# A four-layer stack of attention, feed forward and state space: products with a zero state left out, one output product moved, loads and splits moved

## The chip, the core and the metric

One core of one Trainium2 chip runs the whole program in one launch. Its engines are TensorE (PE; its weight loads are PEld), VectorE (DVE), ScalarE (ACT), GpSimd (POOL) and SyncE (SP), which issues most DMAs. The metric is device time in microseconds (us), the median of several runs; lower is better.

## The reference

Two rows (b = 0, 1) of 1024 tokens by 512 features, float32, go through four layers, each `x = x + layernorm(f(layernorm(x)))`:

```python
att  = softmax(causal(q @ k.T / 4)); out = att @ v @ Wo.T + bo       # 32 heads of 16
ffn0 = lin(silu(lin(x, gate)) * lin(x, up), down)   # lin: w * (su @ sv), rank 4, 1792 wide
# state space: 8 groups of 8 heads of 64, state 128
xBC = silu(conv4(x @ Wx)); dt = softplus(x @ Wdt + dt_bias)
state = state * exp(dt * A) + dt * x * B            # state starts at zero
y = state @ C + x * D
out = (rmsnorm_by_group(y) * norm_weight * silu(x @ Wgate)) @ Wout
ffn1 = (silu(x @ Wg) * (x @ Wu)) @ Wd               # 1376 wide, padded to 11 tiles of 128
```

## The kernel before

**Products.** Most float32 products are three matmuls each: both operands are split into a rounded part ("hi") and a rest ("lo"), and hi·hi, lo·hi and hi·lo are summed in a PSUM bank. Weights come by DMA into a raw tile, ACT or POOL makes the hi part and POOL the lo part.

**Phases.** A loop runs over the two rows. In each, the engines pass the phases ATT, PROJ, FFN0, STEPS_DT, MAMBA and FFN1. An engine that is done with a phase drains and calls `leave`; an engine that calls `enter` waits until all five have left the phase before. Phases reuse SBUF, and that is what `enter` protects. Within a phase, each engine runs its own list of instructions in order, and semaphores connect them; nothing is reordered at run time.

**Attention.** Eight quads of four heads (t = 0 to 7). `attention_order` writes out one list, `ORDER`, that all engines follow. Its first part makes queries and keys ("proj", f = 0 to 3, four 512-token halves each) and values; among them stand "pieces", products of queries and keys for the row maxima of quad 0, which DVE reduces. A projection for f waits for the split of its weights (`wqk_ready`), which waits for their load (`load_qk(f)` in SP's list). Each quad's operands are then copied by 24 DMAs into `stack_q` and `stack_k` (`copy_part`): SP does this for quads 0, 1 and 2 (`stack`), ACT's queue for quad 3 (the "copies" entries). SP's list is: load f=0, 1; stack 0; load f=2; stack 1; wait for the values; ones; stack 2; load f=3; `put_maxima(0)`, two DMAs that bring the turned maxima into `stack_q`. The first score product waits for the latter, and the first exponential on ACT for all of stacks 2 and 3, because they are copied from the `probs` tiles that it writes.

**State space.** STEPS_DT makes the time steps: `steps_in(s)` is the product with Wdt for one half of the tokens, `steps_copy` brings it to SBUF, `steps_turn` turns it, and `decay_sums` forms the running sums. The phase also makes the first conv projections (`project`, `first_conv`, `first_silu`) and the second half of the layer norm (`normed_y`, `add_y`, `moments_x`, `root`, `normed_x`, `norm_turn`, `norm_lo`, in that order of need). SP loads Wdt and the small parameters after `enter(STEPS_DT)`, then `cpar` and the first weight tiles.

MAMBA runs eight groups (g), the middle six in a hardware loop, each in eight chunks of 128 tokens (c). `m_group` in each engine's part has the chunk's list. On PE: the decays, the B and C products into bank 3 (L998, L999), one or two conv projections for the next half or group (two at c = 0 and 2 of each half), into banks 0 and 1 in turn; the product of C with the state ("inter", L1020); the gate product, with the eight head products of the chunk between its matmuls (L959); the out projection of the chunk before (`project_out`, weights `wy`, with four transposes between); and the state's update product (L1046). The two banks of projections and gate are shared: a use waits until the use two before it has been read, a projection by DVE's `convolve`, so the gate of chunk 0 waits for the conv of the first projection. `turned_hi` (ACT, L1257) and `turned_lo` (DVE, L1711) copy the chunk before's normalised result, turned by PE (L940), out of bank 2; `project_out` waits for them. DVE sums y (L1764, L1767), gates it (L1769), adds the out projection to Y (`gather`, L1719) and updates the state (L1788); POOL decays the state (L2078). At the start of a group DVE sets the state to zero (L1739), and chunk 0 goes through the same operations with it as the others.

**Second feed forward.** SP loads its first two tiles after `enter(FFN1)`, POOL splits them, and PE starts with `gate(0, 0, 0)`. The second half of the norm runs beside it: after `moments_x` a `root` on POOL, then `normed_x` on ACT, and PE's `norm_turn` for tokens 4 to 7 stands behind its third product.

## Time and profile before

| | |
|---|---|
| median of 3 runs | 4067.1 us (4065.34 to 4072.07) |
| the profiled execution | 4082.54 us |
| its span | 4080.8 us |
| PE busy, matmuls | 3809.3 us (93%), 18088 |
| DVE busy | 2732.6 us (67%) |
| ACT busy | 1686.5 us (41%) |
| POOL busy | 1805.8 us (44%) |
| mean granted clock | 0.925 of 2.4 GHz |

A span is from the first to the last instruction of one profiled execution. Busy shares are means over phases with different limits. A matmul's end is modelled, so rows overlap a little: the time of a run of matmuls is the distance between two starts. SPq and ACTq are the issue times of DMAs in SP's and ACT's queue.

### The profile page before, as it was taken

How to read it: one execution, taken by the hardware profiler on the slowest of the kernel's cores; microseconds unless marked ns; L12 is line 12 of the kernel's file. 1: busy time of each engine (PE TensorE's matmuls, PEld its weight loads, DVE VectorE, ACT ScalarE, POOL GpSimd, SP SyncE). 2: the span in 40 equal slices, each digit the busy share in tenths (PEclk: the TensorE clock that was granted, in tenths of full speed). 3: DMA queues.
4: the chain of work that ended last, by engine and by line, in shares of the span. 5: the costliest groups of instructions: out<-in, count | busy, mean ns of one | idle time of the engine just before them, and what ended most of it. 6: DMA issues, size and time to landing. Idle time of an engine off the chain costs nothing.

```text
span 4080.8 us, 61636 instructions
## 1 busy us (share of the span) xinstructions
PE 3809.3 (93%) x18088; PEld 2768.1 (68%) x18088; DVE 2732.6 (67%) x5102; ACT 1686.5 (41%) x3555; POOL 1805.8 (44%) x1993
## 2 busy tenths in 40 slices
PE   7899899799999999979979998996999999999797
PEld 5444588577777777767754446874777777777586
DVE  4576455678777787764546754556778777787545
ACT  1344411355555555541214443114555555555412
POOL 2111444266555665643221124433666655665432
PEclk9767799899999999989987768998999999999899
DMA  4120111011010111001051301101111100110111
GB/s 104 31 49 27 34 48 40 24 37 35 29 27 25 31 36 28 23 26 57 24 116 27 61 15 33 48 32 34 27 37 31 31 21 25 36 34 18 52 39 36
DMA packets 84630, 151.95 MB, mean 37 GB/s; under 512 B 16488, under 2 KB 18616, under 8 KB 84432
## 3 DMA queue, kind: packets, MB, share of 16 engines
q1 hardware_dynamic: 80784, 142.23, 13.1%
q10 hardware_dynamic: 3648, 7.34, 0.7%
q8 instruction: 92, 1.51, 0.1%
q14 instruction: 106, 0.87, 0.1%
HBM read 119.37 MB, written 4.19 MB: 30 GB/s over the span
## 4 chain that ended last, share of the span: by engine, by line
PE 81%; issue 7%; DVE 4%; POOL 2%; DVEq 2%; ACT 1%; POOLq 1%; DMA 1%; SPq 1%; ACTq 0%; PEldq 0%; PEld 0%
PE banks L928 30%; PE banks L595 8%; PE banks L596 7%; PE banks L597 7%; PE banks L845 5%; PE banks L959 4%; PE banks L826 4%; PE banks L803 3%; PE banks L1020 2%; PE banks L1046 2%; PE banks L976 1%; PE banks L977 1%; PE banks L949 1%; PE banks L940 1%; DVEq L1690 1%
## 5 line engine op out<-in xcount | busy, mean ns | idle before, releaser
L1687 DVE SCALAR_TENSOR_TENSOR conv<-banks,cpar,conv 128x509 f32<-128x509 f32 (+2 forms) x576 | 428.1, 743 | 123.0 <-ACT conv L1247 106.0
L959 PEld LDWEIGHTS banks<-xdt,decay 128*128 128x128 f32 x2048 | 393.9, 193 | 65.8 <-DVE decay L1706 11.2
L1213 ACT ACTIVATE probs<-banks 128x1024 f32<-128x1024 f32 (+3 forms) x384 | 296.7, 809 | 328.9 <-PE banks L826 328.3
L1474 DVE TENSOR_TENSOR Y<-banks,Y 128x512 f32<-128x512 f32 x368 | 253.1, 691 | 164.3 <-PE banks L597 163.0
L595 PE MATMUL banks<-xhi,f_hi 128*128 128x512 f32 x800 | 325.8, 407 | 30.9 <-POOL f_lo L1891 16.6
L959 PE MATMUL banks<-xdt,decay 128*128 128x64 f32 x2048 | 342.0, 249 | 12.7 <-DVE decay L1706 9.3
L2012 POOL TENSOR_SCALAR_AFFINE_SELECT probs<-probs 128x256 f32<-128x256 f32 x256 | 103.8, 406 | 536.6 <-ACT probs L1213 536.2
L803 PE MATMUL banks<-stack_k,stack_q 48*128 48x512 f32 (+3 forms) x768 | 320.5, 500 | 13.8 <-DVE mx L1607 6.8
L1602 DVE CUSTOM_DVE_ANT_0 banks<-banks,mask_qk 128x128 f32<-128x128 f32 (+3 forms) x512 | 249.3, 500 | 117.7 <-PE banks L803 113.2
L596 PE MATMUL banks<-xhi,f_lo 128*128 128x512 f32 x800 | 320.8, 401 | 0.0
L597 PE MATMUL banks<-xlo,f_hi 128*128 128x512 f32 x800 | 320.6, 401 | 0.0
L928 PE MATMUL banks<-xhi,wx_hi 128*128 128x512 f32 x720 | 310.4, 431 | 0.0
L826 PE MATMUL banks<-stack_q,stack_k 50*128 50x512 f32 (+3 forms) x768 | 292.0, 487 | 5.7 <-DVE mx L1602 3.0
L928 PE MATMUL banks<-xhi,wx_lo 128*128 128x512 f32 x720 | 295.9, 411 | 0.0
L928 PE MATMUL banks<-xlo,wx_hi 128*128 128x512 f32 x720 | 295.5, 410 | 0.0
L826 PEld LDWEIGHTS banks<-stack_q,stack_k 50*128 50x128 f32 x768 | 169.0, 249 | 168.3 <-issue 125.8
L928 PE MATMUL banks<-wg_hi,xhi 128*128 128x512 f32 x512 | 262.0, 512 | 21.8 <-DVE conv L1687 21.8
L2090 POOL TENSOR_SCALAR rg<-ss 128x1 f32<-128x1 f32 x128 | 25.1, 196 | 541.3 <-ACT banks L1321 541.3
L1889 POOL TENSOR_SCALAR f_hi<-f_raw 128x512 fp32r<-128x512 f32 x150 | 96.5, 643 | 324.2 <-PE banks L597 301.9
L928 PE MATMUL banks<-wg_lo,xhi 128*128 128x512 f32 x512 | 238.3, 465 | 0.0
L1132 ACT CAST h_hi<-hf 128x512 fp32r<-128x512 f32 x100 | 62.2, 622 | 408.2 <-DVE hf L1459 408.2
L928 PE MATMUL banks<-wy_hi,yt_hi 128*128 128x512 f32 x512 | 229.4, 448 | 0.7 <-POOL wy_lo L2038 0.7
(229 smaller groups left out, 10402.1 us busy)
## 6 DMA issues: line engine op xcount, KB each, us to landing
m_raw<-in_w_mamba SPq DMA_DIRECT2D x224, 256.0 KB, 2.6
f_raw<-in_w_ffn SPq DMA_DIRECT2D x50, 768.0 KB, 4.6
x_next<-in_x SPq DMA_DIRECT2D x6, 1024.0 KB, 8.8
wqk_raw<-in_w_attn SPq DMA_DIRECT2D x8, 512.0 KB, 3.7
stack_q<-part_hi SPq DMA_DIRECT2D x64, 64.0 KB, 2.4
stack_k<-part_hi SPq DMA_DIRECT2D x64, 64.0 KB, 2.5
X<-in_x SPq DMA_DIRECT2D x4, 1024.0 KB, 6.5
out_y<-X ACTq DMA_DIRECT2D x4, 1024.0 KB, 5.1
```

The source lines that it names most:

```text
L595: pe.matmul(dst, a_hi(kt), w_hi(kt), start=first, stop=False)
L596: pe.matmul(dst, a_lo(kt), w_hi(kt), start=False, stop=False)
L597: return pe.matmul(dst, a_hi(kt), w_lo(kt), start=False, stop=last)
L803: pe.matmul(bank[RING_BANK[use]][:, 0:cols], stack_q[buf][base:base + ROWS, h, i * P:(i + 1) * P], stack_k[buf][base:base + ROWS, h, s * H ...
L826: r = pe.matmul(bank[h][:, at:at + w], stack_k[buf][base:base + ROWS + 2, h, j * P:(j + 1) * P], stack_q[buf][base:base + ROWS + 2, h, s * ...
L845: r = pe.matmul(bank[6][32 * h:32 * h + VW, lo:HALF], V[:, j, QUAD * t + h, :], probs[n % 2][:, h, at:at + w], start=j == 0, stop=j == CPH ...
L928: r = pe.matmul(dst, a(kt), w(kt), start=n == 0, stop=n == 3 * KT - 1)
L959: r = pe.matmul(bank[7][:, h * MP:(h + 1) * MP], decay[:, h, :], xdt[:, h * MP:(h + 1) * MP], start=True, stop=True, skip_group_check=True)
L1213: act.activation(probs[n % 2][:, 2 * p:2 * p + 2, 0:w], banks[:, 2 * p:2 * p + 2, 0:w], ACT.Exp, scale=1.0 / HD ** 0.5).then_inc(exp_done[ ...
L1474: dve.tensor_tensor(Y[:, i, :], bank[6 + i % 2], Y[:, i, :], ALU.add).then_inc(f["dn_used"], 1)
L1602: dve.tensor_tensor_reduce(out=src, in0=src, in1=mask_qk[:, HALF - cols:HALF], scale=1.0, scalar=NEG, op0=ALU.add, op1=ALU.max, accum_out= ...
L1687: r = dve.scalar_tensor_tensor(out=rest, in0=src[:, 0:HALF - lag], scalar=cpar[:, o:o + 1], in1=rest, op0=ALU.mult, op1=ALU.add)
```

## The change

The state space's chunk 0 of each group leaves out the product of C with the zero state, the eight scalings of it on ACT, one of DVE's two sums, the memset and POOL's decay of the state; the state after chunk 0 is a copy of the update product. In chunk 0 of each group but the first, the out projection of the chunk before stands ahead of the gate product, and `turned_hi` and `turned_lo` stand ahead of the first conv. The second feed forward's first two tiles are loaded as soon as the last group's projections are done, and POOL splits the first of them (three matrices) before it leaves MAMBA; tile buffers of the second feed forward lie elsewhere in SBUF for that. Wdt, the small parameters, `cpar` and the first two state space weight tiles are loaded before SP leaves FFN0, and Wdt is split at the end of POOL's FFN0 list. In STEPS_DT some steps change places. In attention, SP's list now has load f=3 right after stack 1 and copies quad 3 too, between stack 2 and `put_maxima(0)`; ACT copies nothing. The weights of queries and keys are split in one piece per f, after the last projection of f-1. The pieces stand four to a block, and a step with the maxima and six pieces stands between projections f=2 and f=3. The core of the diff:

```diff
-    blocks_left = [("values", 3), (1, 0), ("values", 4), (1, 1), ("values", 5), ("values", 6), (1, 2), ("values", 7),
-                   (1, 3), (2, 0), (2, 1), (2, 2), (2, 3), (3, 0), (3, 1), (3, 2), (3, 3)]
-    for at, (first, second) in enumerate(blocks_left):
+    blocks_left = [("values", 3), (1, 0), ("values", 4), (1, 1), ("values", 5), (1, 2), ("values", 6), (1, 3),
+                   ("values", 7), (2, 0), (2, 1), (2, 2), (2, 3), None, (3, 0), (3, 1), (3, 2), (3, 3)]
+    for block_ in blocks_left:
+        if block_ is None:
+            yield "maxima", 0
+            yield from some(2)
+            yield "maxima_out", 0
+            yield from some(AHEAD - 2)
+            continue
+        first, second = block_
...
+        count = min(PER_BLOCK, len(pieces) - (NQ - 1) * NP) if len(pieces) > (NQ - 1) * NP else 0
+        yield from some(min(count, 2))
         yield ("values_out", second) if values else ("proj_lo", first, second)
-        yield from some(count - 2 if count > 2 else 0)
+        yield from some(count - min(count, 2))
...
@@ SyncE, attention @@
         stack(0)
         load_qk(2)
         stack(1)
+        load_qk(3)
         held(sp, v_used, b + 1)
         ones_in(1)
         stack(2)
-        load_qk(3)
+        stack(3)
         put_maxima(0)
         for t in range(1, NQ):
...
@@ SyncE, ffn_loads @@
             load(0, 0, True)
             load(0, 1, True)
             if i == 1:
+                leave(sp, b, MAMBA)
+                enter(sp, b, FFN1)
...
@@ SyncE, end of FFN0 @@
         ffn_loads(0, w_ffn0, NF0, True)
-        leave(sp, b, FFN0)
-        enter(sp, b, STEPS_DT)
-
+        enter(sp, b, FFN0)
         for dst, src in ((wdt_raw[:], w_dt), (dtb[:], dt_bias), (alog[:], a_log), (dsk[:], d_skip)):
             sp.dma_start(dst, src).then_inc(dt_w_in, 16)
-        leave(sp, b, STEPS_DT)
-
+        sp.dma_start(cpar[:], conv_par[0]).then_inc(cpar_in, 16)
...
-        sp.dma_start(cpar[:], conv_par[0]).then_inc(cpar_in, 16)
-        for n in range(CT):
-            m_load(0, n, n, n < 2)
+        for n in range(2):
+            m_load(0, n, n, True)
+        leave(sp, b, FFN0)
+        enter(sp, b, STEPS_DT)
+        for n in range(2, CT):
+            m_load(0, n, n)
+        leave(sp, b, STEPS_DT)
...
         m_group(MG - 1, True)
-        leave(sp, b, MAMBA)
-        enter(sp, b, FFN1)
+        held(sp, proj_done, (b + 1) * PROJ_PER_B)
         ffn_loads(1, w_ffn1, NF1, False)
...
@@ TensorE, attention @@
-                if use_f % 2 == 0 and part == 0:
-                    pe.wait_ge(wqk_ready, b * 8 + 2 * f + which + 1)
+                if use_f == 0 and part == 0:
+                    pe.wait_ge(wqk_ready, b * 8 + 2 * f + 2)
...
@@ TensorE, m_group @@
-                pe.wait_ge(state_ready, it + 1)
-                if c == 0:
-                    pe.wait_ge(inter_used, START + it)
-                pe.matmul(bank[6][:], xbc[s][:, XT + 1, ck], state[:], start=True, stop=True
-                          ).then_inc(inter_done, 1)
+                if c:
+                    pe.wait_ge(state_ready, sm + c)
+                    pe.matmul(bank[6][:], xbc[s][:, XT + 1, ck], state[:], start=True, stop=True
+                              ).then_inc(inter_done, 1)
+
+                def out_ahead():
+                    if c == 1:
+                        pe.wait_ge(m_split, b * (MG * W_PER_G) + g * W_PER_G + W_PER_G)
+                    pe.wait_ge(bc_ready, START + it + 1)
+                    ahead = (c + 1) % CPH != 0
+                    project_out(it - 1, {2 + 2 * k: lambda k=k: turn_x(it + 1, c + 1, k) for k in range(XT)}
+                                if ahead else {})
+
+                if c == 0 and not start:
+                    out_ahead()
...
+                if c:
+                    out_ahead()
 
                 if c < TT - 1:
-                    pe.wait_ge(inter_used, START + it + 1)
+                    pe.wait_ge(inter_used, START + sm + c)
...
@@ TensorE, STEPS_DT @@
-            if ft == 2:
+            if ft == 1:
                 norm_turn(b * 4 + 2, 2, half(1))
                 normed(b * 4 + 2, 1)
                 steps_in(1)
-            if ft == 3:
+            if ft == 2:
                 steps_turn(1)
...
@@ ScalarE, attention, copies @@
-                first, last = arg
-                if first == 0:
-                    held(act, v_used, b + 1)
-                    held(act, part_lo_ready, b * 16 + 8)
-                    act.drain()
-                for n in range(first, last):
-                    copy_part(act, 3, n)
...
@@ ScalarE, m_group @@
+                if c == 0 and not start:
+                    turned_hi(it - 1)
...
                     if not turned_yet:
-                        turned_hi(it - 1)
+                        if c:
+                            turned_hi(it - 1)
...
+                if c:
+                    act.wait_ge(inter_done, START + (b * MG + g) * (TT - 1) + c)
+                    act.wait_ge(gt_ready, (b * MG + g) * 2 + c // CPH + 1)
+                    for h in range(HPG):
+                        own = slice(h * MP, (h + 1) * MP)
+                        r = act.activation(yv[:, own], bank[6][:, own], ACT.Identity, scale=gt[:, EC, c, h:h + 1])
+                    r.then_inc(inter_used, 1)
...
@@ ScalarE, STEPS_DT @@
+        act.wait_ge(dt_w_in, (b + 1) * 64)
+        act.activation(neg_a[:], alog[:], ACT.Exp)
         held(act, cpar_in, (b * MG + 1) * 16)
         for n in range(2):
             split_hi(wx_hi[:, n, :], n, 0)
-        act.wait_ge(dt_w_in, (b + 1) * 64)
-        act.activation(neg_a[:], alog[:], ACT.Exp)
         normed_y(b * 4 + 1, half(1))
         for n in range(2, 4):
             split_hi(wx_hi[:, n, :], n, 0)
         first_conv(0)
+        normed_x(b * 4 + 2, 2, half(1))
         first_conv(1)
         first_tanh(0)
-        normed_x(b * 4 + 2, 2, half(1))
...
@@ VectorE, m_group @@
-            held(dve, inter_done, START + (b * MG + g) * TT)
-            dve.memset(state[:], 0.0).then_inc(state_ready, 1)
...
+                if c == 0 and not start:
+                    turned_lo(it - 1)
+                    turned = True
...
+                if c == 0:
+                    dve.wait_ge(intra_done, START + it + 1)
+                    dve.wait_ge(pool_x, START + it + 1)
+                    dve.tensor_tensor(yv[:], xd[:], bank[7], ALU.add).then_inc(y_ready, 1)
...
+                if c == 0:
+                    dve.wait_ge(st_mm, START + sm + 1)
+                    dve.tensor_copy(state[:], bank[6]).then_inc(state_ready, 1)
...
@@ VectorE, STEPS_DT @@
+        steps_copy(0)
         add_y(b * 4 + 1, half(1))
         moments_x(b * 4 + 1, 1)
-        steps_copy(0)
         first_conv(0)
+        norm_lo(b * 4 + 2, half(1))
         first_conv(1)
         first_silu(0)
-        norm_lo(b * 4 + 2, half(1))
...
@@ GpSimd, ffn @@
-        split_one(0, 0, 0)
         if i == 0:
+            split_one(0, 0, 0)
             root(PRE, e, 0)
             split_one(0, 0, 1)
             root(POST, e - 1, 1)
-        else:
-            split_one(0, 0, 1)
         split_one(0, 1, 0)
         root(PRE, e, 1)
         split_one(0, 1, 1)
-        split_one(0, 0, 2)
+        if i == 0:
+            split_one(0, 0, 2)
...
+        if i == 0:
+            held(pool, dt_w_in, (b + 1) * 64)
+            split(wdt_hi[:], wdt_lo[:], wdt_raw[:]).then_inc(dt_w_ready, 1)
...
@@ GpSimd, attention @@
-                    held(pool, ring_done, b * RING + RING_ENDS.index(("proj", f - 1, 2 * which + 1)) + 1)
-                split(wqk_hi[:, which, :], wqk_lo[:, which, :], wqk_raw[:, which, :]).then_inc(wqk_ready, 1)
+                    held(pool, ring_done, b * RING + RING_ENDS.index(("proj", f - 1, 3)) + 1)
+                split(wqk_hi[:], wqk_lo[:], wqk_raw[:]).then_inc(wqk_ready, 2)
...
@@ GpSimd, m_group @@
-                    pool.wait_ge(state_ready, it + 1)
-                    pool.wait_ge(inter_done, START + it + 1)
-                    pool.tensor_tensor(by_head(state[:]), by_head(state[:]), per_head(gt[:, ED, c, :]),
-                                       ALU.mult).then_inc(state_dec, 1)
+                    if c:
+                        pool.wait_ge(state_ready, sm + c)
+                        pool.wait_ge(inter_done, START + sm + c)
+                        pool.tensor_tensor(by_head(state[:]), by_head(state[:]), per_head(gt[:, ED, c, :]),
+                                           ALU.mult).then_inc(state_dec, 1)
...
@@ GpSimd, end of MAMBA @@
+        f = F[1]
+        held(pool, f["raw_in0"], b * ((NF1 + 1) // 2) * 16 + 16)
+        for m in range(3):
+            split(*(w[0][:, m, :] for w in (wf1[1], wf1[2], wf1[0]))).then_inc(f["w_ready"], 1)
...
```

## Rows read from the trace of the kernel before

**Rows 1.** The page: chain of waits that ended last, by engine, share of the span
```profile
PE 81%; issue 7%; DVE 4%; POOL 2%; DVEq 2%; ACT 1%; POOLq 1%; DMA 1%; SPq 1%; ACTq 0%; PEldq 0%; PEld 0%
```

**Rows 2.** Windows: start:end, us, busy of PE, PEld, DVE, ACT, POOL, clock, DMA, GB/s
```profile
820.00:1768.00 948.00, 931.37 (x4628) 725.10 (x4627) 744.10 (x1156) 506.77 (x1269) 577.24 (x577) 1.00 0.11 29
200.00:250.00 50.00, 48.09 (x255) 22.61 (x247) 34.52 (x109) 21.36 (x30) 8.53 (x21) 0.66 0.21 34
```

**Rows 3.** PE's waits, 813 to 1826 us: who waited for whom, total us, times, longest
```profile
PE banks L928 <- DVE conv L1687: 10.9, 7, 1.6
```

**Rows 4.** Timeline, chunk 0 of a middle group: start us, us, what [idle before <-releaser]
```profile
949.80 0.27 PE L940 MATMUL banks<-ident,yn 128*128 128x128 f32 x1
...
950.76 0.58 ACT L1257 CAST yt_hi<-banks 128x512 fp32r<-128x512 f32 x1
950.89 0.80 DVE L1684 SCALAR_TENSOR_TENSOR conv<-carry,cpar,conv 128x3 f32<-128x3 f32 x1 [1.36 <-ACT conv L1247]
...
952.70 1.02 PE L1020 MATMUL banks<-state,xbc 128*128 128x512 f32 x2
...
955.03 0.68 DVE L1711 TENSOR_TENSOR yt_lo<-banks,yt_hi 128x512 fp32r<-128x512 f32 x1
955.30 0.49 PE L928 MATMUL banks<-wg_hi,xhi 128*128 128x512 f32 x1 [1.58 <-DVE conv L1687]
...
959.90 0.48 PE L928 MATMUL banks<-wy_hi,yt_hi 128*128 128x512 f32 x1
...
963.21 1.02 PE L1046 MATMUL banks<-xw,b_tm 128*128 128x512 f32 x2
...
965.00 0.27 PE L998 MATMUL banks<-ident,xbc 128*128 128x128 f32 x1
```

**Rows 5.** Timeline, end of FFN0 to the start of MAMBA, first row
```profile
757.57 0.69 DVE L1434 TENSOR_TENSOR xlo<-banks,xhi 128x512 fp32r<-128x512 f32 x1 [0.24 <-ACT xhi L1116]
...
761.53 0.16 DVE L1413 TENSOR_SCALAR var_eps<-mv 128x4 f32<-128x4 f32 x1
761.74 0.66 PE L595 MATMUL banks<-xhi,wdt_hi 128*64 128x512 f32 x1 [4.82 <-POOLq L277]
...
765.46 0.81 ACT L1098 ACTIVATE Y<-Y,shift,rstd 128x512 f32<-128x512 f32 x1 [0.47 <-POOL shift L1899]
...
779.57 1.51 ACT L1112 ACTIVATE xn<-X,shift,rstd 128x512 f32<-128x512 f32 x2
...
786.22 0.44 PE L595 MATMUL banks<-xhi,wdt_hi 128*64 128x512 f32 x1 [1.40 <-DVE xlo L1434]
...
813.71 0.66 PE L949 MATMUL banks<-ident,xbc 128*128 128x128 f32 x2 [7.98 <-DVE xbc L1696]
```

**Rows 6.** Timeline, end of MAMBA to the third product of FFN1, first row
```profile
1826.91 0.69 DVE L1719 TENSOR_TENSOR Y<-banks,Y 128x512 f32<-128x512 f32 x1 [3.00 <-PE banks L928]
...
1835.18 0.79 PE L595 MATMUL banks<-xhi,f_hi 128*128 128x512 f32 x1 [8.31 <-POOL f_lo L1891]
...
1841.20 1.52 ACT L1112 ACTIVATE xn<-X,shift,rstd 128x512 f32<-128x512 f32 x2 [0.40 <-POOL shift L1899]
...
1847.50 0.48 PE L595 MATMUL banks<-xhi,f_hi 128*128 128x512 f32 x1
```

**Rows 7.** Timeline, attention of the first row up to its first exponential
```profile
86.07 1.79 SPq L309 DMA_DIRECT2D stack_q<-probs  x3
...
102.57 0.38 SPq L461 DMA_DIRECT2D wqk_raw<-in_w_attn  x1
...
110.40 0.79 PE L595 MATMUL banks<-xhi,wqk_hi 128*128 128x512 f32 x1 [7.33 <-POOL wqk_lo L1891]
...
128.10 1.02 ACT L1213 ACTIVATE probs<-banks 128x1024 f32<-128x1024 f32 x1 [2.50 <-PE banks L826]
```

**Rows 8.** Tile stack_q, 0 to 150 us: its copies, from issue to landing
```profile
DMA to landing us min/median/max: 2.2/2.5/4.0
```

**Rows 9.** Timeline of POOL: the rest part of a split, 2048 columns
```profile
26.18 4.52 POOL L1891 TENSOR_TENSOR wv_lo<-wv_raw,wv_hi 128x2048 fp32r<-128x2048 f32 x1
```

More of the change, by code:

```diff
@@ L536, in ffn_loads @@
                     for par in range(2):
-                        load(1, par, split=w_place(par, 2) + 1)
+                        load(1, par, split=w_place(i, par, 2) + 1)
                     with sp.Fori(2, n // 2) as p:
@@ L1031, in m_group @@
                         at += 1
-                        if not start:
-                            if c == 1:
-                                pe.wait_ge(m_split, b * (MG * W_PER_G) + g * W_PER_G + W_PER_G)
-                            pe.wait_ge(bc_ready, START + it + 1)
-                            ahead = (c + 1) % CPH != 0
-                            project_out(it - 1, {2 + 2 * k: lambda k=k: turn_x(it + 1, c + 1, k) for k in range(XT)}
-                                        if ahead else {})
+                        if c:
+                            out_ahead()
                         if c < TT - 1:
-                            pe.wait_ge(inter_used, START + it + 1)
+                            pe.wait_ge(inter_used, START + sm + c)
                             pe.wait_ge(pool_x, START + it + 1)
@@ L1310, in m_group @@
                         act.wait_ge(yn_ready, START + it)
-                        act.wait_ge(inter_done, START + it + 1)
-                        act.wait_ge(gt_ready, (b * MG + g) * 2 + c // CPH + 1)
-                        for h in range(HPG):
-                            own = slice(h * MP, (h + 1) * MP)
-                            r = act.activation(yv[:, own], bank[6][:, own], ACT.Identity, scale=gt[:, EC, c, h:h + 1])
-                        r.then_inc(inter_used, 1)
+                        if c:
[5 more added lines that the diff above has]
+                            r.then_inc(inter_used, 1)
                         act.wait_ge(gate_done, START + it + 1)
```

124 lines of the change are left out of this document (65 added, 59 removed).

## The prediction, made before the change was run

> **What bounds the kernel now.** I read the chain of waits first: 81% of the span is TensorE (PE) [rows 1], so the question for each edit is how much PE time or PE waiting it takes away. The windows come second: over most of the state space layer's eight groups PE is busy 931 of 948 us at the full clock, while DVE has 744 and POOL 577 [rows 2]. So there an edit pays only through PE. PE's own waits say where its idle time is: seven waits of 1.6 us for a conv, 10.9 us in the first row [rows 3], one for each group that has a group before it. The timelines then give the three places where PE stands still for long: before the time step product [rows 5], at the start of the second feed forward [rows 6], and between projections f=2 and f=3 in attention [rows 7].
>
> **State space, chunk 0.** Before, PE starts the zero state's product at 952.70 and the gate product at 955.30, 2.60 us later: the product, then 1.58 us of waiting for the conv of the first projection, whose bank the gate wants. Gate and heads take 959.90 - 955.30 = 4.60 us, the out projection 963.21 - 959.90 = 3.31 us [rows 4]. In the new order the out projection starts at 952.70 if the turned result is ready. The last transpose (949.80 + 0.27) ends at 950.07; ACT's 0.58 us copy now goes first (to about 950.75), DVE's 0.68 us (L1711) follows to 951.5: 1.2 us early. The out projection ends at 956.0. The conv is pushed back: it started at 950.89 and was done at 955.3, when it let PE go; now it starts near 951.6, behind the two copies, and is done near 955.9, still in time. Gate and heads run to 960.6, and the state's update follows at 960.6 instead of 963.21: 2.6 us less. Something is late next: the B product (965.00 before, 1.79 us after L1046, so 962.4 now) needs bank 3, which DVE frees with `gather`, after y (0.7), gate (0.7) and gather (0.7) in a row from the heads' end, 960.5: 962.7 (DVE's gather took 0.69 [rows 6]). That gives back 0.3. Net 2.3 us in 14 groups (seven per row): 32 us. The two first groups have no out projection to move and wait for the decay there; one sum less on DVE (0.7 us) gives perhaps 0.5 each: 1 us. ACT's eight scalings, the memset and POOL's state decay cost nothing by themselves, since PE covers them. Sum 33 us. Bounds: at best 2.6 x 14 + 1 = 37; at worst the out projection waits for the copies as long as before (955.03 + 0.68 = 955.7) and the gate's cover is gone: 3.0 lost against 2.6 won, 6 us slower in all.
>
> **End of FFN0 to MAMBA.** PE has the tokens it needs at 757.57 + 0.69 = 758.3 but starts the time step product at 761.74, when the late-loaded Wdt is split [rows 5]. Now load and split lie under the last tiles of FFN0: 3.4 us. The longer gain is behind it, and it is a chain, not a wait of PE. DVE's variance is ready at 761.7 as before, but POOL has the first weight split behind it by then, so root and `normed_y` start near 763.1 instead of 765.46 (2.3 us). Then `steps_copy(0)` no longer follows `moments_x`; and the turn of the second half of the tokens stands after the second projection, not the third. With `moments_x` 2.3 us earlier, root and `normed_x` are due near 771.2 instead of 779.57, which stood behind a conv step; from there to the product four tiles take 786.22 - 779.57 = 6.7 us, so the second time step product starts near 777.9: 8.3 us. Behind it the order is one dependent series to the first turn of MAMBA at 813.71 (sums, decays, convs on a DVE without gaps), which moves as a whole. I take 8.3 per row, 16.6 in all. Bounds: 3.4 per row if only the load's wait goes (7); 10 per row (20) if fewer pauses also keep PE at the full clock.
>
> **Start of the second feed forward.** PE could start after DVE's last gather, 1826.91 + 0.69 = 1827.6, and starts at 1835.18 [rows 6]: 7.2 us if nothing else holds it, for the tiles now come some 50 us ahead, and POOL's three splits (about 6 us) lie beside the last out projection. But the third product and the turn of tokens 4 to 7 need `normed_x`, which starts at 1841.20, at the end of a chain through DVE, POOL and ACT that the change doesn't touch. PE will wait there, and the fourth product, at 1847.50 before, also needs a split that POOL starts after that chain's root (1841.2 + 2.0 = 1843.3). So of 7.2 us some 3 are given back: 4.2 per row, 8.4 in all. Bounds 3 and 7.2 per row.
>
> **Attention.** Load f=3 is no longer behind 24 copies, so the 7.33 us that PE waited at 110.40 [rows 7] mostly go: f=3's split (its rest part took 4.52 us for 2048 columns [rows 9], so some 2.3 for 1024, and 3.5 with the hi part, an estimate) begins when f=2's projections end, near 102, and six pieces lie beside it. The four projections that follow are 48 matmuls of 0.23 us or somewhat more (the out projection's twelve, with four transposes between, took 3.31 [rows 4]), so PE would be at the scores near 117 instead of 125. But SP's queue takes its place. Before, 24 copies took 102.57 - 86.07 = 16.5 us of SP's time, 0.69 each [rows 7], and ACT issued the other 24 at the same time. Now both sets and load f=3 are in series: f=2's weights are split whole (3.5 us) before that load may go, so stack 2 starts near 89.6 instead of 86.1, stack 3 ends near 121 to 122, and the maxima, issued behind it, land 2.5 us later [rows 8]: first score 124 to 125, first exponential near 125.3 instead of 128.10. I take 2.9 in the first row. In the second, PE also waits for the first whole split, which costs 1.5 us more than the half before, an estimate, of which DVE's memset hides some: 0.8, net 2.1. Sum 5 us. Bounds: 4 us slower (each copy at 0.75 us, row 2's split in full) and 8 faster.
> Here the Trainium skill says otherwise (DMA: Bandwidth & Descriptors, section "Issuing engines are not separate DMA queues"): starting DMAs from several engines "will only save the time on the sequencer", which is usually small against the transfer. By these rows the time on the sequencer, 24 times 0.69 us, is what counts here, since the 2.5 us to land overlap; what the rule would give is rival C.
>
> **Sum.** 33 + 16.6 + 8.4 + 5 = 63 us, from the profiled execution's 4082.5 (span 4080.8 and 1.7 around it) to 4019.5. The runs' median, 4067.1, lies 15.4 us below the profiled one, so 4067.1 - 63 = 4004.
>
> **Rivals.** A: the loop keeps its wait. If the out projection ahead of the gate only swaps which thing PE waits for (yt copies, bank 3, the heads), each group gains the product alone, 1.0 us: 16 us at most instead of 33, 4021. For: the margins are 1.2 us and 0.1 us. Against: DVE was idle 1.36 us before that conv [rows 4]. 10%.
> B: the transitions give only the waits for loads, 3.4 and 3 us per row: 13 instead of 25, 4016. For: in both places a norm chain of DVE, POOL and ACT is what ends last. 10%.
> C: SP's queue is not what ends last, because the copies issue faster there than before or PE is late by itself: the scores start when PE is there, near 117, the first exponential near 119 instead of 128.10, 9 us per row instead of 2.5, 13 more in all: 3991. Against: the 24 issues in 16.5 us [rows 7]. 6%.
> D, slower: PE's clock. Where PE pauses often, as in the scores, the granted clock is 0.66, in the loop 1.00 [rows 2]. If the new order in chunk 0, or a PE that waits 7 us for SP's queue before the scores, let a stretch of the loop fall to 1.2 GHz, each us of matmul would become about 1.8: the change is slower from 63 / 0.83 = 76 us of matmuls on, a clock of 0.96 or less over the loops of both rows. With a tenth of the loop (190 us) at the lower level it would be 4004 + 158 = 4162. Against: the change takes pauses out of the loop and adds none over 0.3 us. 3%.
> That the change doesn't do what it says: the conv wait could stay because ACT's first conv step now follows its copy; that is A.
>
> **Chances.** The forecast has 71%, A 10, B 10, C 6, D 3. The range: C's 3991 and a little below for a full 37 and 20, so 3989; upward A and B together would be 4033, so 4030. About 0.2% (8 us) is what a measurement of this kernel can tell from no change. Faster than that 95%; within 2%, if A, B and the bad end of attention meet; slower 3%.
>
> **What would show it.** Right: no PE wait for a conv at the gate of chunk 0, an out projection before it, a group shorter by 2.3 us; the second time step product about 8 us earlier against the end of FFN0; PE's third FFN1 product followed by a wait for `normed_x`; in attention no wait at f=3 but one before the first score, released by the maxima's DMA. Wrong: waits for L1257 or L1711 at the moved out projection, a clock under 1.00 in the loop, or a first exponential as late as before.

## The result, and the profile after

The changed kernel takes 4003.9 us (median of four runs, 4001.1 to 4019.5), the kernel before beside it 4069.6 (four runs, 4065.3 to 4074.1): ratio 0.9846, 95% interval 0.9818 to 0.9875. The forecast was 4004, range 3989 to 4030. Timed again later, in six runs, it took 4004.0 against 4069.3. The interval means a gain of 51 to 74 us, so a forecast that meets the median within 0.1 us is in that closeness luck; the stages below say more.

The profiled execution took 4001.1 us, span 3999.3, 81.5 less in span than that of before. The page's chain of waits has less PE [rows 1]:

```profile
PE 78%; issue 7%; POOL 5%; DVE 4%; SPq 2%; POOLq 2%; ACT 1%; DVEq 1%; DMA 0%; ACTq 0%
```

I cut both rows of every trace at the same five instructions, all from timelines. Lengths in us, row 1 / row 2; "groups" is the distance of one group's first product of chunk 1's out projection from the next group's, in the middle groups. The last exponential is taken at the start of its timeline row, which mostly holds two, so the second and third column carry 0.3 to 0.4 us of that.

| kernel | first projection to first exponential | first to last exponential | on to last xlo of FFN0 | on to first turn of MAMBA | on to end of row | groups |
|---|---|---|---|---|---|---|
| before | 98.0 / 99.3 | 311.2 / 308.0 | 318.2 / 318.2 | 56.1 / 56.2 | 1242.4 / 1242.9 | 124.8 |
| changed | 96.1 / 96.8 | 298.6 / 302.6 | 316.6 / 316.5 | 49.4 / 49.5 | 1221.1 / 1221.6 | 122.9 |
| changed_again | 95.3 / 96.9 | 298.0 / 301.7 | 316.6 / 316.7 | 49.4 / 49.5 | 1225.2 / 1221.7 | 122.9 |
| old_order | 95.2 / 96.8 | 295.1 / 295.8 | 316.6 / 316.6 | 49.5 / 49.5 | 1244.9 / 1245.5 | 126.2 |
| product_back | 96.2 / 96.2 | 305.0 / 307.6 | 318.8 / 318.2 | 50.3 / 49.5 | 1225.7 / 1225.2 | 123.8 |
| copies_behind | 95.2 / 95.7 | 295.1 / 299.0 | 316.7 / 316.6 | 49.5 / 49.5 | 1249.6 / 1249.1 | 126.0 to 129.0 |
| steps_order | 95.4 / 96.5 | 305.0 / 291.9 | 316.6 / 316.5 | 53.7 / 53.6 | 1221.2 / 1220.7 | 122.9 |
| wdt_late | 96.6 / 96.9 | 302.8 / 291.8 | 318.6 / 318.7 | 54.0 / 54.0 | 1221.7 / 1222.0 | 122.9 |
| ffn1_late | 96.9 / 96.6 | 310.1 / 302.1 | 318.2 / 316.6 | 49.5 / 49.4 | 1225.4 / 1225.6 | 123.0 |
| attention_old | 98.2 / 99.7 | 299.0 / 311.6 | 316.5 / 318.2 | 49.5 / 49.5 | 1221.1 / 1221.8 | 123.0 |
| attention_old_2 | 98.5 / 99.2 | 302.8 / 304.1 | 316.5 / 319.0 | 49.5 / 49.5 | 1221.4 / 1221.6 | 122.9 |
| copies_act | 91.6 / 91.1 | 306.3 / 309.6 | 319.0 / 318.2 | 49.5 / 49.5 | 1221.5 / 1221.7 | 122.9 |
| gather_early | 91.9 / 91.2 | 295.6 / 303.3 | 316.6 / 318.0 | 49.4 / 49.5 | 1221.1 / 1221.7 | 122.9 |
| best | 92.8 / 92.2 | 299.2 / 292.5 | 316.5 / 319.4 | 50.6 / 51.0 | 1221.1 / 1220.6 | 122.9 |

Read it by columns. Where nothing was edited, the groups and the fourth column repeat within 0.3 us (one 50.3 apart), the first within 2. The third is 316.5 to 316.7 or 318.0 to 319.4. The fifth is 1221 to 1222 but for one row (1225.2). It is firm only as a whole: with the same code the layer's last group takes 98.0 us in half of the rows and 99.6 in the others (101.2 in that one), by a short stretch at the lower clock level, and what follows the last out projection takes 224.7 to 225.3 or 221.7 to 222.7. How much of a gain there belongs to the loop and how much to the second feed forward, two profiles can't say. The scores (second column) take 291.8 to 311.6 us whatever the edit. Of the 81.5 us between the profiles, 4.5 lie before the first exponential, 18.0 in the scores, 3.3 in the third column, 13.5 between the layers and 42.6 from there to the ends of the rows (start 0.4 later). The first, fourth and fifth column, the places that the change edits, sum to 60.6; forecast were 63. The medians are 65.7 apart.

**Chunk 0** of a middle group, in a timeline of the changed kernel [rows 4]:

```profile
1048.88 0.27 PE L955 MATMUL banks<-ident,yn 128*128 128x128 f32 x1
1049.19 0.59 ACT L1271 CAST yt_hi<-banks 128x512 fp32r<-128x512 f32 x1 [1.95 <-PE banks L955]
1049.81 0.69 DVE L1730 TENSOR_TENSOR yt_lo<-banks,yt_hi 128x512 fp32r<-128x512 f32 x1 [1.31 <-ACT yt_hi L1271]
...
1051.75 0.39 PE L943 MATMUL banks<-wy_hi,yt_hi 128*128 128x512 f32 x1
...
1055.00 0.39 PE L943 MATMUL banks<-wg_hi,xhi 128*128 128x512 f32 x1
...
1059.50 1.08 PE L1067 MATMUL banks<-xw,b_tm 128*128 128x512 f32 x2
...
1060.91 0.68 DVE L1738 TENSOR_TENSOR Y<-banks,Y 128x512 f32<-128x512 f32 x1
...
1061.64 0.14 PEld L1014 LDWEIGHTS banks<-ident,xbc 128*128 128x128 f32 x1 [0.56 <-DVE Y L1738]
...
1071.29 0.50 PE L943 MATMUL banks<-wy_hi,yt_hi 128*128 128x512 f32 x1 [0.27 <-POOL wy_lo L2067]
```

The out projection (1051.75) has no wait in brackets, its operand being done at 1050.50, 1.25 us early; nor has the gate (1055.00). From the last transpose to the B product's transpose (its matmul starts at 1061.65) it is 1061.65 - 1048.88 = 12.77 us, against 965.00 - 949.80 = 15.20: 2.43 less. The new wait for bank 3 is there: from the state's update (L1067) to that transpose 2.15 us instead of 1.79, behind DVE's gather. One wait that I had not named stands in chunk 1, 0.27 for POOL's rest part of the out weights. A group is 1.8 to 2.2 us shorter, 2.0 on the mean of 14, and the layer, from first turn to the end of its last out projection, 996.3 instead of 1013.2 in row 1.

**FFN0 to MAMBA**, timeline, row 1 [rows 5]:

```profile
741.84 0.69 DVE L1452 TENSOR_TENSOR xlo<-banks,xhi 128x512 fp32r<-128x512 f32 x1 [0.24 <-ACT xhi L1137]
742.58 0.69 PE L608 MATMUL banks<-xhi,wdt_hi 128*64 128x512 f32 x1 [1.40 <-DVE xlo L1452]
...
747.36 2.93 ACT L1119 ACTIVATE Y<-Y,shift,rstd 128x512 f32<-128x512 f32 x4 [2.96 <-POOL shift L1927]
...
755.75 1.52 ACT L1133 ACTIVATE xn<-X,shift,rstd 128x512 f32<-128x512 f32 x2 [3.17 <-POOL shift L1927]
...
756.62 1.36 PE L636 MATMUL banks<-ident,xn 128*128 128x128 f32 x8 [2.33 <-ACT xn L1133]
...
762.44 0.69 PE L608 MATMUL banks<-xhi,wdt_hi 128*64 128x512 f32 x1 [1.40 <-DVE xlo L1452]
...
763.78 0.63 PE L608 MATMUL banks<-xhi,wdt_hi 128*64 128x512 f32 x1
...
791.25 1.09 PE L964 MATMUL banks<-ident,xbc 128*128 128x128 f32 x4 [8.01 <-DVE xbc L1715]
```

Against the last xlo, the first product starts at 0.74 instead of 4.17, `normed_y` at 5.5 instead of 7.9, `normed_x` at 13.9 instead of 22.0, the second product at 20.6 instead of 28.7, the first turn at 49.4 instead of 56.1. So 8.1 us are won at the second product and 6.7 are left: its first matmuls take 0.63 us apiece, 0.39 to 0.44 before, and the product 4.1 us instead of 2.8; PE had stood 2.33 and 0.78 us a few us before, where it had stood 1.38 in the kernel before.

**Start of FFN1** [rows 6] and **attention** [rows 7], timelines, row 1:

```profile
1787.62 0.69 DVE L1738 TENSOR_TENSOR Y<-banks,Y 128x512 f32<-128x512 f32 x1 [2.49 <-PE banks L943]
...
1788.65 0.49 PE L608 MATMUL banks<-xhi,next_hi 128*128 128x512 f32 x1 [1.07 <-DVEq L290]
...
1799.45 0.69 DVE L1478 TENSOR_TENSOR hf<-sg,banks 128x512 f32<-128x512 f32 x1 [0.35 <-issue]
...
1800.19 0.79 PE L608 MATMUL banks<-xhi,f_hi 128*128 128x512 f32 x1 [5.77 <-DVE hf L1478]
...
1805.47 1.48 PE L636 MATMUL banks<-ident,xn 128*128 128x128 f32 x8
```

```profile
91.31 1.79 SPq L482 DMA_DIRECT2D stack_q<-probs  x3
...
106.02 0.28 PE L825 MATMUL banks<-ident,mx 128*32 128x128 f32 x1 [3.90 <-DVE mx L1631]
...
108.00 0.79 PE L608 MATMUL banks<-xhi,wqk_hi 128*128 128x512 f32 x1
...
121.48 0.40 PE L610 MATMUL banks<-xlo,wqk_hi 128*128 128x512 f32 x1
...
122.86 0.52 SPq L489 DMA_DIRECT2D stack_q<-mt_hi  x1
...
125.79 0.49 PE L841 MATMUL banks<-stack_q,stack_k 50*128 50x512 f32 x1 [3.91 <-DMA stack_q<-mt_lo]
126.58 1.94 ACT L1227 ACTIVATE probs<-banks 128x1024 f32<-128x1024 f32 x2 [3.97 <-PE banks L841]
```

FFN1's first product starts 1.0 us after the gather instead of 8.3, then PE stands 5.8 us at the third, for a DVE that has the norm's sums to do first. In attention the 7.33 us at f=3 are gone (3.9 are left before it, for DVE's maxima), and 3.9 stand before the first score, for the maxima's DMA behind SP's 48 copies (91.31 to 122.68, 0.65 each).

### The profile page after: what moved, and what is told of

Same layout as the page of the kernel before. It is cut to its first block, busy times and chain, and to the rows that moved or that the text cites. A ratio compares the mean times of both kernels' runs of the same rounds, so it can differ in the third digit from the quotient of the medians.

```text
span 3999.3 us, 61384 instructions
## 1 busy us (share of the span) xinstructions
PE 3759.2 (94%) x18056; PEld 2740.2 (69%) x18056; DVE 2681.8 (67%) x5070; ACT 1664.1 (42%) x3427; POOL 1788.6 (45%) x1961
## 4 chain that ended last, share of the span: by engine, by line
PE 78%; issue 7%; POOL 5%; DVE 4%; SPq 2%; POOLq 2%; ACT 1%; DVEq 1%; DMA 0%; ACTq 0%
PE banks L943 29%; PE banks L608 8%; PE banks L610 7%; PE banks L609 7%; PE banks L860 4%; PE banks L974 4%; PE banks L841 4%; PE banks L818 3%; PE banks L1067 2%; PE banks L1035 2%; POOL wy_lo L2067 2%; SPq L482 1%; PE banks L964 1%; PE banks L991 1%; PE banks L992 1%
## 5 line engine op out<-in xcount | busy, mean ns | idle before, releaser
L841 PE MATMUL banks<-stack_q,stack_k 50*128 50x512 f32 (+3 forms) x768 | 283.4, 475 | 12.7 <-DMA stack_q<-mt_lo 9.5
L608 PE MATMUL banks<-xhi,f_hi 128*128 128x512 f32 x608 | 247.1, 406 | 20.9 <-DVE hf L1478 14.9
L610 PE MATMUL banks<-xlo,f_hi 128*128 128x512 f32 x608 | 243.0, 400 | 0.0
L609 PE MATMUL banks<-xhi,f_lo 128*128 128x512 f32 x608 | 242.5, 399 | 0.0
L943 PE MATMUL banks<-wg_hi,xlo 128*128 128x512 f32 x512 | 225.2, 440 | 0.0
```

The source lines that it names most:

```text
L608: pe.matmul(dst, a_hi(kt), w_hi(kt), start=first, stop=False)
L609: pe.matmul(dst, a_lo(kt), w_hi(kt), start=False, stop=False)
L610: return pe.matmul(dst, a_hi(kt), w_lo(kt), start=False, stop=last)
L841: r = pe.matmul(bank[h][:, at:at + w], stack_k[buf][base:base + ROWS + 2, h, j * P:(j + 1) * P], stack_q[buf][base:base + ROWS + 2, h, s * ...
L943: r = pe.matmul(dst, a(kt), w(kt), start=n == 0, stop=n == 3 * KT - 1)
```

## The experiments

All are edits of the changed kernel unless said otherwise. The runs of one kernel scatter by 10 us and more; stage lengths from a profile, by a few tenths. Each verdict rests on the stage.

**old_order: chunk 0 in its old order, the product left out.**

```diff
-if c == 0 and not start: out_ahead()          # PE, ahead of the gate
-if c: out_ahead()                             # PE, behind the gate
+if not start: out_ahead()
-if c == 0 and not start: turned_hi(it - 1)    # ACT; DVE's turned_lo likewise
```

> The changed kernel with chunk 0 in its old order: out projection behind the gate, turned result's copies at their old places; the zero state's product stays away. Theory (the product alone buys nothing, because PE then waits the longer for the conv): one wait of 1.58 + 1.02 = 2.6 us at the gate of chunk 0 in seven groups per row, seen under the conv; a group takes 125.0 us as before (122.9 in the changed kernel), the state space layer 1012 to 1013 us per row (996.3 changed, 1013.2 before), the kernel some 31 us more, 4035. Rival A (the product is what counts, the wait stays at 1.6): 124.0 us per group, 16 us more in all, 4020.

4050.5 us; a group 126.2 us, 1.4 longer than before though a product shorter. PE's waits between 830 and 1760 us, a timeline of one gate, and windows of the pause and the 3.4 us behind it:

```profile
PE banks L943 <- DVE conv L1700: 17.4, 8, 2.5
```

```profile
1053.46 0.49 PE L943 MATMUL banks<-wg_hi,xhi 128*128 128x512 f32 x1 [2.47 <-DVE conv L1700]
...
1054.28 0.63 PE L943 MATMUL banks<-wg_hi,xhi 128*128 128x512 f32 x1
...
1056.26 0.77 PE L943 MATMUL banks<-wg_hi,xhi 128*128 128x512 f32 x1
...
1059.62 0.48 PE L943 MATMUL banks<-wy_hi,yt_hi 128*128 128x512 f32 x1
```

```profile
1051.00:1053.46 2.46, 0.00 (x1) 0.01 (x1) 2.38 (x5) 0.93 (x2) 2.46 (x3) 1.00 0.23 69
1053.46:1056.90 3.44, 3.44 (x12) 2.90 (x13) 3.29 (x7) 0.48 (x1) 1.23 (x2) 0.61 0.33 103
```

And the same two windows of the kernel before:

```profile
953.72:955.30 1.58, 0.00 (x1) 0.01 (x1) 1.51 (x4) 0.19 (x2) 1.58 (x2) 1.00 0.46 137
955.30:958.00 2.70, 2.70 (x16) 2.35 (x16) 2.62 (x5) 2.11 (x9) 2.23 (x3) 1.00 0.43 114
```

The wait grew as the theory says, from 1.58 to 2.47 us, so the product alone buys nothing. What neither theory had: behind 2.47 us of standing the granted clock is 0.61, mostly its lower level of 1.2 GHz, and gate and heads take 59.62 - 53.46 = 6.2 us; behind 1.58 us it is 1.00 and they take 4.6. It is so in all 14 groups: the low stretch stands behind each pause, in none of the 14 of the kernel before. The product had kept PE busy through a wait; without it the clock falls behind the pause, and that costs 1.6 us per group.

**product_back: a product of that shape returned, in the new order.**

```diff
+else:   # c == 0, ahead of the out projection; another moving operand, the result is not used
+    ...
+    pe.matmul(bank[6][:], xbc[s][:, XT + 1, ck], xbc[s][:, XT, :], start=True, stop=True)
```

> The changed kernel with a product of the zero state's shape (128x128 by 128x512) put back into chunk 0 ahead of the out projection, its result unused. Theory: with the out projection ahead PE has no wait left that could hide it; a group grows by the product's 1.02 us less the 0.3 us that PE now waits for wy_lo in chunk 1, so 0.7 us in 14 groups and 1.0 in two, 12 us more in all, 4016. Without that give-back 16 us, 4020. Rival: other waits of the new order (bank 3, heads) hide it as the conv did before: under 4 us.

4024.4 us; a group 123.8, 0.9 more than changed (0.7 expected); the layer 1003.5 / 1003.1 against 996.3 / 996.4, 14 us in all (12 expected). To the ends of the rows only 8 us of it are left (fifth column), since here the stretch behind the last out projection is the shorter of its two lengths (222.2 us). With old_order this makes a table of two by two, us per group (the first is the kernel before, which also has the scalings, the memset and the decay): old order with the product 124.8, without 126.2; new order with it 123.8, without 122.9. The move is worth 1.0 with the product in place and 3.3 without; leaving the product out costs 1.4 in the old order and gains 0.9 in the new. Neither part can be priced alone.

**copies_behind: out projection ahead, the copies of the turned result behind the first conv as before** (only the ACT and DVE lines of old_order).

> The changed kernel with the out projection ahead of the gate in chunk 0, but the two copies of the turned result behind the first conv again, where they were. Theory: DVE's copy is done some 3 us after PE has finished the projections, so PE waits 2.9 us at the out projection, seven times a row, and as in old_order such a pause lets its clock fall afterwards, about 1.5 us more: a group takes 122.9 + 2.9 + 1.5 = 127.3 us, the kernel 62 us more, 4065. Without the clock's fall 125.8 and 4045. Rival: the copy comes as early as DVE allows (it was idle before that conv), wait under 1 us, 123.9.

4069.6 us, ratio to before 1.0005 (0.9983 to 1.0026): the whole gain of the change is gone. The layer takes 30.7 us more per row than in the changed kernel, 61 in all, as expected (62). PE's waits, 830 to 1760 us, a timeline,

```profile
PE banks L943 <- DVE yt_lo L1727: 21.1, 7, 3.0
```

```profile
1055.27 0.77 PE L943 MATMUL banks<-wy_hi,yt_hi 128*128 128x512 f32 x1 [3.02 <-DVE yt_lo L1727]
...
1061.22 0.39 PE L943 MATMUL banks<-wg_hi,xhi 128*128 128x512 f32 x1
```

and windows: the 9.2 us up to the pause, the 5.2 behind it, and the 5.2 behind the same pause two groups later:

```profile
1043.00:1052.20 9.20, 9.20 (x46) 7.19 (x44) 6.41 (x9) 5.76 (x11) 7.57 (x8) 1.00 0.18 57
...
1055.27:1060.50 5.23, 5.23 (x14) 3.87 (x15) 3.71 (x7) 0.00 (x0) 0.68 (x1) 0.50 0.16 49
...
1311.68:1316.91 5.23, 5.23 (x27) 4.23 (x28) 3.69 (x7) 0.00 (x0) 0.66 (x1) 1.00 0.16 45
```

A wait of 3.0 us, and behind it a clock of 0.50, the level of 1.2 GHz: the out projection takes 5.95 us instead of 3.3. But this is so in the first three of a row's seven groups alone (127.7 to 129.0 us each); in the other four the same wait of 3.0 us leaves the clock at 1.00, and the group takes 125.9 to 126.3. So length alone doesn't decide whether the clock falls; what does, no run here shows. Against before (124.8), 1.3 us per group come without any fall of the clock, and the fall adds 12 us over both rows. Two lines on ACT and DVE decide whether the move on PE wins 2 us per group or loses as much.

**steps_order: the old order between the layers, Wdt still early** (PE turns the second half after the third projection; ACT's `normed_x` behind conv 1; DVE's `steps_copy(0)` behind `moments_x`).

> The changed kernel with the old order of the steps between the two layers (second half of the tokens turned after the third projection, ACT's normed_x behind the second conv, DVE's copy of the steps behind moments_x); Wdt stays loaded and split early. Measured from the last xlo of the first feed forward: first time step product at 0.74, second at 20.6, first turn of the state space layer at 49.4 (changed); 4.2, 28.7, 56.1 (before). Theory (a dependent chain that the order lengthens): 0.74, about 26.3, 53.8, so 4.4 us per row and 8.8 in all, near 4013. Rival B (only the wait for Wdt counted): the first turn stays within 1 us of 49.4 and the time at 4004.

First product at 0.74, second at 26.1, first turn at 53.7 us: as the theory said, within 0.2. The time didn't come as expected, 4003.5 instead of 4013: its four runs lie between 3990.8 and 4014.7, and in the profiled one (4002.9) the scores of row 2 took 291.9 us, 10.7 less than in the changed kernel's.

**wdt_late: Wdt loaded and split late, the new order kept.**

```diff
-    split(wdt_hi[:], wdt_lo[:], wdt_raw[:]).then_inc(dt_w_ready, 1)   # POOL, in FFN0's last tiles
+    split(wdt_hi[:], wdt_lo[:], wdt_raw[:]).then_inc(dt_w_ready, 1)   # POOL, in STEPS_DT; SP's loads too
```

> The changed kernel with Wdt, the two vectors and the skip loaded and split at the start of the step stage again, the new order of the steps kept. Theory: first time step product at 4.2 us after the last xlo (0.74 changed), normed_y 2.4 us later, second product at 23.0 (20.6), first turn at 51.8 (49.4): 2.4 us per row, 4.8 in all, near 4009; the 3.4 us at the first product aren't all seen at the end. Rival B: the 3.4 us are the whole gain: first turn at 52.8 to 56.1, the order being worth nothing.

4011.1 us; first product at 4.28, second at 24.9, first turn at 54.0: the first as expected, the rest 2 us later. A timeline tells why:

```profile
752.68 0.66 PE L608 MATMUL banks<-xhi,wdt_hi 128*64 128x512 f32 x1 [4.93 <-POOLq L290]
...
755.42 2.94 ACT L1119 ACTIVATE Y<-Y,shift,rstd 128x512 f32<-128x512 f32 x4 [4.07 <-POOL shift L1927]
...
757.33 0.68 DVE L1824 COPY dt_turned<-banks 64x512 f32<-64x512 f32 x1 [3.21 <-PE banks L610]
757.93 3.59 DVE L1459 TENSOR_TENSOR X<-X,Y 128x512 f32<-128x512 f32 x4
```

`normed_y` starts at 755.42, but DVE's additions wait behind `steps_copy(0)`, which waits for PE's product (757.33). The new order puts that product on the norm's chain. So the two parts help each other. From before (56.1) the new order alone gains 2.1 us per row (54.0), the early Wdt alone 2.5 (53.7), both together 6.7 (49.4). In both runs `cpar` and the first two weight tiles stay loaded early; their share wasn't tested.

**ffn1_late: FFN1's first tiles loaded after MAMBA and split in the old order.**

> The changed kernel with the second feed forward's first two tiles loaded after the state space layer, and split in the old order, as before. Theory: PE's first product starts some 8.3 us after the last out projection (1.1 changed), but most of that is slack, since PE waits 5.8 us at the third product: the turn of the later tokens comes at 19.8 us after the out projection (17.9 changed, 16.9 in other profiles), so 2 to 3 us per row; the rest of the feed forward (205.3 to 207.3 us changed, 209.4 and 210.0 before) stays at 205 to 207 if its size goes by where the tiles lie and by the clock, or goes back to 209 if it comes from the early start. In all 4 to 9 us, 4008 to 4013.

4014.8 us; the first product starts 8.3 us after the last out projection, the turn of the later tokens at 19.7. To the end of row (fifth column) it takes 1225.4 / 1225.6 us against 1221.1 / 1221.6: 4.2 us per row, the forecast's 4.2. From the last out projection alone it is 226.0 / 226.5 against 222.3 / 222.4 in copies_act, whose last group has the same length (99.6 us), 3.9 per row.

**attention_old and attention_old_2: the whole attention of before.**

> The changed kernel with the attention of the kernel before (order of pieces and copies, load f=3 behind stack 2, stack 3 issued by ACT, split of f in two halves). Theory: only the stretch from the first projection to the first exponential changes, from 96.1 and 96.8 us (rows 1 and 2) back to about 98.0 and 99.3, so 4.5 us in all, 4008; the scores (first to last exponential: 298.6 and 302.6 us changed, 311.2 and 308.0 before) go by the granted clock alone and fall somewhere in 298 to 311 whichever attention runs. Rival: the new order itself shortens the scores by what the two profiles differ, 18 us, and then this kernel has 308 to 311 in both rows and takes 4026.

> The changed kernel with the attention of before once more, timed in the same rounds as the changed one. If the order of attention is worth the 2 to 3 us up to the first exponential alone, the medians differ by 4 to 5 us, and the scores fall anywhere in 291 to 312. If the old order also keeps the scores at the lower clock: 307 us in both rows, and 16 us between the medians.

> The changed kernel once more, with a profile, beside the next run. Open is whether the new order in attention also makes the scores themselves shorter: first to last exponential took 291.8 to 310.1 us, 301.5 on the mean, in 16 rows with the new order, and 299.0 to 311.6, 307.5 on the mean, in four rows with the old one. If only the granted clock decides: both orders spread alike, here within 291 to 312. If the order counts, some 6 us per row: 301 here.

First exponential at 98.2 / 99.7 and 98.5 / 99.2 us: 2.4 and 2.9 us later than the mean of the eight other profiles with the changed attention (95.9 / 96.6). That much is settled. The scores are not. The windows of both rows in one execution of attention_old, same code:

```profile
128.46:427.47 299.01, 287.61 (x1529) 128.56 (x1528) 197.79 (x616) 147.66 (x191) 57.30 (x128) 0.72 0.17 34
2114.21:2425.83 311.62, 300.14 (x1529) 132.53 (x1528) 198.14 (x616) 147.74 (x190) 57.29 (x128) 0.68 0.16 33
```

and the shortest but one of all, in steps_order:

```profile
2118.46:2410.36 291.90, 278.06 (x1529) 124.00 (x1527) 196.91 (x615) 147.71 (x191) 57.53 (x128) 0.76 0.18 35
```

ACT, POOL and DVE are busy the same time in all three, PE is not: the length goes with the granted clock, over all 28 rows with a correlation of -0.94. Over 6 rows with the old attention the mean is 306.1 us (standard deviation 5.0), over 22 with the new 300.4 (5.6), 5.7 less with a standard error of 2.4. The medians of attention_old_2 and changed_again, timed together, are 13.0 us apart (4017.0, 4004.0), of which 5.3 lie before the first exponential. Whether the new order also lifts the clock in the scores by some 5 us a row, or 6 rows are too few, stays open.

**copies_act: stack 3's copies issued by ACT.**

```diff
+if first == 2: yield "copies", 6 * second, 6 * second + 6     # ORDER, behind each proj_hi of f=2
-stack(3)                                                      # SP
```

> The changed kernel with stack 3's 24 copies issued by ACT again, six behind each eviction of f=2, while load f=3 stays early and the order of pieces is the new one. Theory (SP's queue is what ends last before the scores): SP ends stack 2 near 107.5, ACT's copies near 106, the maxima land near 110, and PE goes from the last projection, 121.9, into the scores: first exponential near 123.2 instead of 126.6, 3.3 us per row, 6.6 in all, 3997. Rival 1: ACT's issuing (24 of 0.65 us) pushes its evictions of f=2 back and with them the maxima and f=3's projections: nothing won or some us lost. Rival 2 (issue is not the limit, the copies themselves are): both queues then get slower, above 1 us per copy, and the first exponential stays near 126.6.

3998.4 us (3997.6 to 4010.3), ratio to before 0.9813 (0.9797 to 0.983). First exponential at 91.6 / 91.1 us, 4.3 and 5.5 earlier than 95.9 / 96.6; 3.3 were expected. Timeline:

```profile
105.39 1.89 ACTq L322 DMA_DIRECT2D stack_k<-probs  x3
...
107.94 0.52 SPq L500 DMA_DIRECT2D stack_q<-mt_hi  x1
...
121.30 0.50 PE L851 MATMUL banks<-stack_q,stack_k 50*128 50x512 f32 x1
...
122.07 1.02 ACT L1245 ACTIVATE probs<-banks 128x1024 f32<-128x1024 f32 x1
```

Both queues issue a copy every 0.7 us side by side (24 in 16.8 us on SP, in 16.6 on ACT), and PE enters the scores without a wait. ACT's evictions of f=2 come up to 1.4 us later than in the changed kernel, and the start of the scores doesn't show it. The Trainium skill (DMA: Bandwidth & Descriptors, section "Issuing engines are not separate DMA queues") calls the sequencer's time "usually small relative to the DMA itself"; for one copy the rows agree, 0.65 us of issue against 2.5 to land, but not for the changed kernel's series: 48 issues take 31.4 us, and the landings overlap.

**gather_early: copies_act, and in chunk 0 DVE's gather ahead of y** (one line moved).

> The changed kernel with stack 3's copies issued by ACT (as in copies_act), and in chunk 0 DVE's gather of the out projection's result moved ahead of y, so that bank 3 is free before the B product wants it. Theory: the 0.4 us wait of the B product's transpose in chunk 0 goes, and a group takes 122.5 us instead of 122.9: 5 us less in 14 groups, near 3994. Rival: the wait moves on to wy_lo in chunk 1 (0.3 us now, then 0.7), and a group stays at 122.9.

3998.3 us; a group 122.9: the rival. The B product's transpose no longer waits long, but PE then waits for ACT's x_tm ahead of the next transposes:

```profile
1056.83 0.33 PE L965 MATMUL banks<-ident,yn 128*128 128x128 f32 x1 [0.36 <-ACT x_tm L1315]
```

**best: copies_act, and the second half's steps turned before the third projection** (one line moved).

> The changed kernel with stack 3's copies on ACT (as in copies_act) and, between the layers, PE's turn of the second half of the time steps ahead of the third projection instead of behind it. Theory: the turn starts when DVE's copy is there, 67.4 instead of 69.4 us after 700, so time step sum, decays and the first turn of the state space layer come 1.7 to 2 us earlier (47.6 us after the last xlo instead of 49.4), 3.5 in all beside the 9 to 10 of copies_act: 3995 to 3991. Rival: the pause of 0.9 us that PE then has, or the conv it delays, takes it back: first turn at 49 or later.

3994.9 us (0.9821, 0.9794 to 0.9848). The turn's sum starts 1.8 us earlier after the second product, but conv 2 comes later, DVE stands 3.15 us for it, and the first turn is at 50.6 / 51.0 instead of 49.4: the rival. What makes this kernel quicker is the copies (92.8 / 92.2). Three kernels with ACT's copies took 3998.4, 3998.3 and 3994.9, the changed one 4003.9 and 4004.0; by the stage it is 9.8 us. The medians' 5.5 us are within their scatter; the stage isn't, so copies_act is the better kernel as far as the stages go.

## Why the prediction was right, and where it wasn't

The mechanism held in all four places, and the terms are near. That the median came out at 4003.9 against 4004 is luck all the same: the stages gave 60.6 us and not 63, the medians 65.7, and inside the terms misses cancel.

- **Loop, 33 us: 33.6 measured** (first turn to last out projection, 16.8 per row). The out projection waits for nothing, the wait at the gate is gone, bank 3 gives back 0.36 (0.3). But the 14 groups gave 27.6 us and not 32: chunk 0 wins 2.43, and 0.5 of that is lost again before the next group, in part to waits for POOL's rest part (1.5 us in five of them in row 1), so a group wins 2.0 and not 2.3. Start and last group gave 6.0 us for both rows instead of 1, and part of that is the clock: other profiles of the same loop have a last group 1.6 us longer and a layer of 999 us, and would have given 28. Only loop and second feed forward together are firm: 42.6 us, forecast 41.4.
- **FFN0 to MAMBA, 16.6: 13.5.** That the second time step product starts 8.3 us earlier held (8.1). "Behind it the order is one dependent series to the first turn of MAMBA [...] which moves as a whole" failed: the product runs at the lower clock, 4.1 us instead of 2.8. I had thought of the clock only as a gain from fewer pauses; PE, waiting for `normed_x` in the new order, got one more. Rival B fell: order and load both count.
- **FFN1, 8.4: 9.0 between the two profiles, 8.3 by ffn1_late.** The third product did wait, but for DVE's `hf`, queued behind the norm's sums, not for `normed_x`; another releaser, the same chain.
- **Attention, 5: 4.5** between the profiles, 5.3 by attention_old and its repeat. SP's queue was the bound; copies_act shows it by taking it away.
- **The bounds of the loop failed.** A late copy was to make it "6 us slower in all" at worst: copies_behind's layer takes 1027.0 us against 1013.1, 28 us slower in all. The bound gave 0.4 us per group for the longer wait; the groups whose clock stayed at 1.00 lose 1.3, since bank 3 and POOL's rest part take their share here too, and the fall of the clock adds 12 us. Rival A gave the product alone up to 16 us of gain: old_order's layer takes 1020.3, 14 us more. There the wait grew by 0.9 of the product's 1.0 us, and the clock fell behind it in every group. Rival D had that mechanism, but looked for it only in the forecast order, which has no such pause.
- **Scores: not in the sum.** Whether the edits touch them stays open (attention_old), and 18 of the 81.5 us between the two profiles lie there. The profiled execution of before is 13 us above its median, that of the changed kernel 3 below: a difference of two profiles would have credited the change with 24% more than the medians do, and the sum over edited stages does not.
- **The range.** Its lower end doesn't follow from its own words: C's 3991 with a full 37 and 20 is 3984 and not 3989.

## What to carry to other kernels

Removing work pays only where nothing else ends last; where PE waits anyway, the removed product was filling the wait, and a pause grown from 1.6 to 2.5 us cost more in clock than it saved in work. So price a longer PE wait at its length and, as a case of its own, at what follows it at the lower clock. When a loop is reordered on one engine, its operands' producers have to move with it: two lines on ACT and DVE carried the loop's whole gain. Compare kernels by stages cut at the same instructions, and set aside those whose length follows the granted clock.

## What I had not expected of the hardware

- A pause of 1.4 to 1.6 us before the gate left the clock at 1.00 in all 14 groups; one of 2.3 to 2.5 us brought it down in all 14 (0.61 over the 3.4 us behind one of 2.47). One of 3.02 us brought it to 0.50 over 5.2 us, though PE had been busy 9.2 of 9.2 us before that pause, but only in 6 of 14 groups; in 8 it left it at 1.00. In the last group PE waits 2.1 us for the state: of the 26 rows of the edited kernels 13 have a stretch at the lower level behind it and 13 don't, two rows of one execution (changed_again) among them. A pause's length alone doesn't tell the clock behind it.
- The same 1529 matmuls of the scores, PE about 95% busy, took 291.8 to 311.6 us at granted clocks of 0.77 to 0.68, differing between two rows of one execution by up to 13 us; the state space layer's middle groups, at a clock of 1.00, repeat within 0.3 us.
- Two engines' queues issue small SBUF to SBUF copies side by side at nearly the rate of one alone: 24 copies take 16.8 us of SP's queue beside ACT's, 16.2 alone.
